# Layer norm's scale through memory: a fused graph network kernel that drops the transposes of h

## The chip, the cores and the metric

One core of one Trainium2 chip. The metric is the device time of one execution in microseconds. All tensors are fp32; matmuls take fp32r operands, and each product is built of three of them (high times high, high times low, low times high).

## The reference, cut to what matters

64 graphs of 128 nodes with 128 channels. `x` is (64, 128, 128), `adj` a mask.

```python
def _layernorm(x, axis=-1, eps=1e-05):
    m = jnp.mean(x, axis=axis, keepdims=True)
    v = jnp.var(x, axis=axis, keepdims=True)
    return (x - m) / jnp.sqrt(v + eps)

h = jnp.maximum(_layernorm(x, axis=-1), 0.0)
return x + gnn(h, adj, ...)

# gnn(x, mask): d = 128
xc = transpose(x, (0, 2, 1))
h = relu(bn1(conv1d(xc, conv1_w, 0)))               # kernel width 1
h = bn2(conv1d(h, conv2_w, 8))                      # 17 taps along the nodes
x_conv = transpose(relu(h + xc), (0, 2, 1))
s = x @ w_se.T + b_se                               # 3 columns
sq = sum(s * s, axis=-1)
A = exp(-(sq[:, :, None] + sq[:, None, :] - 2 s s^T)) * mask
msg = relu(x @ w_msg.T + b_msg)
x_nmp = einsum('bnm,bmd->bnd', A, msg)
gi = concat([x_conv, x_nmp]) @ w_ih.T + b_ih
gh = x @ w_hh.T + b_hh
r = sigmoid(gi_r + gh_r); z = sigmoid(gi_z + gh_z)
n = tanh(gi_n + r * gh_n)
return (1 - z) * n + z * x
```

## The kernel before

The 64 graphs go through in 8 groups of 8 (`NG`, `GB`). Within a group everything is kept turned: channels on the partitions, and 1024 columns (`GW`), node by node with the 8 graphs inside. A group is cut into two halves of 512 columns, the index `c`. Each engine's program is written out by hand, in order, with waits on semaphores; nothing is planned by a compiler. The tail of group g overlaps the head of group g + 1.

Layer norm starts from `xin` (nodes on partitions, 8 tiles of 128x128). VectorE forms `stats` (L715) and `mv` (L722), GpSimd the inverse deviation as a power and its product with the negative mean (`ln_scale`, L348 to L353), ScalarE the normalized rows `hn` in eight passes (`ln_rows`, L449). TensorE turns them (`h_transpose`, L1148, four transposes for each half, into banks 6 and 3 from group 2 on), and ScalarE evicts the banks with a ReLU: once to `h_hi` and once to `hf` (`h_rows`), and by graphs to `hg` (`by_graphs`). VectorE forms `h_lo = hf - h_hi` (`h_low`).

The 17-tap convolution is cut into nine sub-convolutions, `sub_conv(g, 0)` to `sub_conv(g, 8)`, on differences of the input (`level1`, `level2_b`, `level2_u`, in `u`, `vtb`, `vtu`, split to `v_hi` and `v_lo`). ScalarE evicts every third to `mbs` (`m_shared`), VectorE joins the others to it (`join_b`, `add_h`, `add_shared`, `join_y`); their banks are free for the next sub-convolution when that is done. Distances: the three columns of s are split and arranged in `slots` (`distances`, on GpSimd from group 1 on), TensorE turns these (`factor_transposes`, L1189) and multiplies them (`distance`), ScalarE takes the exponential, VectorE applies the mask (`masked`, L888), TensorE gathers (`gather`, L1212). Gates follow, and `update` on VectorE: four passes that also add `x_t`, held in `xt`.

TensorE's order in a group g of the loop:

```python
sub_conv(g, 0); factor_transposes(g); sub_conv(g, 1); distance(g)
sub_conv(g, 2) ... sub_conv(g, 5)
gather(g, 0, 5); h_transpose(g + 1, 0, 6); sub_conv(g, 6)
gather(g, 1, 7); h_transpose(g + 1, 1, 3)
sub_conv(g, 7); sub_conv(g, 8); gates_h(g, 0, ahead)
conv1(g + 1, 0, 0); conv1(g + 1, 1, 7); gates_n(g, 0); gates_xc(g, 0)
gates_h(g, 1, ahead); messages(g + 1); gates_n(g, 1); gates_xc(g, 1)
```

(In group 1 `factor_transposes` and `distance` stand two sub-convolutions later.) The first group also splits the weights into `wt_hi` on ScalarE and `wt_lo` on VectorE, lot by lot, with sums of taps in between, and TensorE runs 25 matmuls on zeros before its first work. All transfers but one are issued by SP in the order of its program.

Of the kernel before, what the change touches and what calls it, by code (L numbers as in the profile page):

```python
# [60 lines left out]
def gnn_kernel(nc, x_nm, x_t, adj_t, w_in, w_conv, w_gate, par_in, row_in, bias_in, out):  # L61
    ctx = ExitStack()
    with ctx:
# [3 lines left out]
        def sem(name):  # L67
# [14 lines left out]
        msg_raw = sb("msg_raw", [P, 9, P])  # L82
# [5 lines left out]
        hn = sb("hn", [P, GB, P])  # L88
# [4 lines left out]
        nmean = sb("nmean", [P, GB])  # L93
        nmr = sb("nmr", [P, GB])
        hf = [sb(f"hf{i}", [P, GW]) for i in range(2)]
# [28 lines left out]
        xt = sb("xt", [P, GW])  # L124
# [6 lines left out]
        w2 = sb("w2", [P, TAPS, P])  # L131
        wg = early[:, 0:9 * P].rearrange("p (k c) -> p k c", c=P)
# [7 lines left out]
        x_landed, xh_landed, wa_landed, w2a_landed, w2b_landed, wg_landed, par_landed, row_landed, bias_landed, xt_landed, mask_landed = (  # L140
            sem("x_landed"), sem("xh_landed"), sem("wa_landed"), sem("w2a_landed"), sem("w2b_landed"),
            sem("wg_landed"), sem("par_landed"), sem("row_landed"), sem("bias_landed"), sem("xt_landed"), sem("mask_landed"))
# [9 lines left out]
        stats_ready, mv_ready, pool_ln, rstd_ready, hn_ready = (  # L152
            sem("stats_ready"), sem("mv_ready"), sem("pool_ln"), sem("rstd_ready"), sem("hn_ready"))
# [124 lines left out]
        def _(sp):  # L278
            sp.dma_start(xin[:, 0:4, :], x_nm[0, :, 0:4, :]).then_inc(xh_landed, 16)
            sp.dma_start(xin[:, 4:8, :], x_nm[0, :, 4:8, :]).then_inc(x_landed, 16)  # L280
# [4 lines left out]
            sp.dma_start(row_raw[0:1, :], row_in).then_inc(row_landed, 16)  # L285
            sp.dma_start(row_raw[32:33, :], row_in).then_inc(row_landed, 16)
            sp.dma_start(bias[:], bias_in).then_inc(bias_landed, 16)
            sp.dma_start(mask[:], adj_t[0]).then_inc(mask_landed, 16)
            for g in range(NG):
                if g + 1 < NG:  # L290

                    sp.wait_ge(hn_ready, NCH * (g + 1))
                    if g < 2:
                        sp.wait_ge(hn_first, g + 2)
                    sp.dma_start(xin[:], x_nm[g + 1]).then_inc(x_landed, 16)

                upto(sp, sum_ready, NCH * g)
                sp.dma_start(xt[:], x_t[g]).then_inc(xt_landed, 16)
                if g > 0:
                    for c in range(NCH):  # L300
# [13 lines left out]
        def _(pool):  # L314
# [27 lines left out]
            def ln_scale(g):  # L342
# [3 lines left out]
                if g == 2:  # L346
                    pool.wait_ge(hn_first, 3)
# [48 lines left out]
        def _(act):  # L396
# [47 lines left out]
            def ln_rows(g):  # L444
# [3 lines left out]
                for j in range(GB):  # L448
                    last = act.activation(hn[:, j, :], xin[:, j, :], ACT.Identity, bias=nmr[:, j:j + 1],  # L449
                                          scale=rstd[:, j:j + 1])  # L450
                    if j % 4 == 3:
                        last.then_inc(hn_ready, 1)
# [1003 lines left out]
```

## Time and profile before

| | us |
|---|---|
| median of 3 runs | 294.5 (294.43 to 295.43) |
| the profiled execution, its time | 294.47 |
| the profiled execution, its span | 292.7 |
| TensorE matmul busy | 281.6 (96%) |
| VectorE busy | 234.9 (80%) |
| ScalarE busy | 181.4 (62%) |
| GpSimd busy | 62.7 (21%) |
| mean granted TensorE clock | 0.996 |

The span is what the profile covers, from the first to the last instruction; the time of an execution has some 1.8 us around it. Busy time of matmuls is latency in a pipeline: the distance between their starts tells what they cost. Group g = 4 starts at 157.02 us with its first sub-convolution.

### The profile page before, as it was taken

How to read it: one execution, taken by the hardware profiler on the slowest of the kernel's cores; microseconds unless marked ns; L12 is line 12 of the kernel's file. 1: busy time of each engine (PE TensorE's matmuls, PEld its weight loads, DVE VectorE, ACT ScalarE, POOL GpSimd, SP SyncE). 2: the span in 40 equal slices, each digit the busy share in tenths (PEclk: the TensorE clock that was granted, in tenths of full speed). 3: DMA queues.
4: the chain of work that ended last, by engine and by line, in shares of the span. 5: the costliest groups of instructions: out<-in, count | busy, mean ns of one | idle time of the engine just before them, and what ended most of it. 6: DMA issues, size and time to landing. Idle time of an engine off the chain costs nothing.

```text
span 292.7 us, 5392 instructions
## 1 busy us (share of the span) xinstructions
PE 281.6 (96%) x1914; PEld 254.6 (87%) x1914; DVE 234.9 (80%) x529; ACT 181.4 (62%) x331; POOL 62.7 (21%) x128
## 2 busy tenths in 40 slices
PE   8779899999999999999999999999999999999993
PEld 6579886999889998899889998899988998899993
DVE  6898988987699668996599776996689966986565
ACT  2776368858656677538765576557674486561362
POOL 7210020540016300460005500361005500140000
PEclk9999999999999999999999999999999999999998
DMA  7700022017000610035000630017000420013001
GB/s 246 301 4 1 0 75 72 0 18 273 2 0 2 223 63 4 0 89 200 0 2 0 168 122 0 2 29 256 5 1 2 143 74 0 0 30 118 2 0 72
DMA packets 6942, 19.03 MB, mean 65 GB/s; under 512 B 898, under 2 KB 1412, under 8 KB 6916
## 3 DMA queue, kind: packets, MB, share of 16 engines
q1 hardware_dynamic: 6772, 18.69, 19.4%
q8 instruction: 15, 0.25, 0.3%
q14 instruction: 11, 0.09, 0.1%
q10 hardware_dynamic: 144, 0.01, 0.0%
HBM read 14.50 MB, written 4.19 MB: 64 GB/s over the span
## 4 chain that ended last, share of the span: by engine, by line
PE 84%; DVE 9%; ACT 3%; issue 1%; POOL 1%; DVEq 0%; POOLq 0%; ACTq 0%
PE ps L1125 23%; PE ps L1127 23%; PE ps L1126 23%; PE ps L1178 4%; PE ps L1212 4%; PE ps L1326 3%; PE ps L1148 2%; DVE wt_lo L735 1%; ACT wt_hi L415 1%; PE ps L1189 1%; PE ps L1202 1%; ACT cp L468 1%; POOL rstd L340 1%; DVE stats L715 1%; DVE vtb L785 1%
## 5 line engine op out<-in xcount | busy, mean ns | idle before, releaser
L1125 PE MATMUL ps<-v_hi,wt_hi 128*128 128x256 f32 x320 | 92.8, 290 | 4.4 <-DVE v_lo L801 3.0
L1127 PE MATMUL ps<-v_hi,wt_lo 128*128 128x256 f32 x320 | 90.0, 281 | 0.0
L1126 PE MATMUL ps<-v_lo,wt_hi 128*128 128x256 f32 x320 | 89.7, 280 | 0.0
L1125 PEld LDWEIGHTS ps<-v_hi,wt_hi 128*128 128x128 f32 x320 | 60.2, 188 | 6.0 <-issue 5.2
L1126 PEld LDWEIGHTS ps<-v_lo,wt_hi 128*128 128x128 f32 x320 | 60.4, 189 | 0.3
L1127 PEld LDWEIGHTS ps<-v_hi,wt_lo 128*128 128x128 f32 x320 | 60.1, 188 | 0.0
L254 POOL CAST slots<-s_sb 128x48 fp32r<-128x48 f32 x7 | 1.6, 228 | 147.3 <-DVE s_sb L873 135.9
L449 ACT ACTIVATE hn<-xin,nmr,rstd 128x128 f32<-128x128 f32 x48 | 19.2, 482 | 13.4 <-POOL nmr L353 13.4
L1125 PE MATMUL ps<-h_hi,wt_hi 128*128 128x512 f32 (+1 forms) x67 | 26.3, 392 | 0.3 <-DVE h_lo L742 0.2
L1127 PE MATMUL ps<-h_hi,wt_lo 128*128 128x512 f32 (+1 forms) x67 | 25.8, 386 | 0.0
L1126 PE MATMUL ps<-h_lo,wt_hi 128*128 128x512 f32 (+1 forms) x67 | 25.8, 385 | 0.0
L566 ACT ACTIVATE gate<-ps,par 128x512 f32<-128x512 f32 x14 | 9.7, 690 | 23.2 <-PE ps L1127 23.2
L844 DVE TENSOR_TENSOR y<-y,mbs 128x512 f32<-128x512 f32 x16 | 11.0, 687 | 14.4 <-ACT mbs L505 14.2
L852 DVE SCALAR_TENSOR_TENSOR y<-ps,par,y 128x256 f32<-128x256 f32 x32 | 14.9, 481 | 7.9 <-PE ps L1127 7.0
L1125 PE MATMUL ps<-n_hi,wt_hi 128*128 128x512 f32 (+1 forms) x51 | 20.0, 392 | 0.0
L1127 PE MATMUL ps<-n_hi,wt_lo 128*128 128x512 f32 (+1 forms) x51 | 19.6, 385 | 0.0
L1127 PE MATMUL ps<-xc_hi,wt_lo 128*128 128x512 f32 (+1 forms) x51 | 19.6, 385 | 0.0
L1126 PE MATMUL ps<-n_lo,wt_hi 128*128 128x512 f32 (+1 forms) x51 | 19.4, 381 | 0.0
L1126 PE MATMUL ps<-xc_lo,wt_hi 128*128 128x512 f32 (+1 forms) x51 | 19.4, 381 | 0.0
L1125 PE MATMUL ps<-xc_hi,wt_hi 128*128 128x512 f32 (+1 forms) x51 | 19.4, 381 | 0.0
L859 DVE SCALAR_TENSOR_TENSOR xc_lo<-y,xc_hi 128x512 fp32r<-128x512 f32 x16 | 10.4, 689 | 10.2 <-ACT xc_hi L554 10.2
L560 ACT ACTIVATE gn<-ps,par 128x512 f32<-128x512 f32 x15 | 10.3, 689 | 11.8 <-PE ps L1127 11.7
(158 smaller groups left out, 644.8 us busy)
## 6 DMA issues: line engine op xcount, KB each, us to landing
mask<-adj_t SPq DMA_DIRECT2D x8, 512.0 KB, 3.3
xt<-x_t SPq DMA_DIRECT2D x8, 512.0 KB, 4.0
out<-gate SPq DMA_DIRECT2D x15, 256.0 KB, 4.1
xin<-x_nm SPq DMA_DIRECT2D x7, 512.0 KB, 3.7
w<-w_conv SPq DMA_DIRECT2D x1, 576.0 KB, 6.7
gate<-w_gate SPq DMA_DIRECT2D x1, 576.0 KB, 7.7
xin<-x_nm SPq DMA_DIRECT2D x2, 256.0 KB, 2.9
w<-w_conv SPq DMA_DIRECT2D x1, 512.0 KB, 5.7
```

The source lines that it names most:

```text
L449: last = act.activation(hn[:, j, :], xin[:, j, :], ACT.Identity, bias=nmr[:, j:j + 1], scale=rstd[:, j:j + 1])
L560: act.activation(gn[c][:], bank(3), ACT.Identity, bias=par[:, HN:HN + 1], scale=0.5).then_inc(ghn_ready, 1)
L566: act.activation(gr[c], bank(4), ACT.Tanh, bias=par[:, HR:HR + 1], scale=0.5).then_inc(r_ready, 1)
L844: dve.tensor_tensor(y_at(s), y_at(s), mbs[1 + s][:].rearrange("p (l b) -> p l b", b=GB).unsqueeze(2).broadcast_to([P, QUART, 2, GB]), ALU. ...
L852: dve.scalar_tensor_tensor(out=at, in0=quarter(1 + t), scalar=par[:, SC2:SC2 + 1], in1=at, op0=ALU.mult, op1=ALU.add).then_inc(y_ready, 1)
L859: dve.scalar_tensor_tensor(out=xc_lo[:, cols(c)], in0=y[:, cols(c)], scalar=0.0, in1=xc_hi[:, cols(c)], op0=ALU.max, op1=ALU.subtract).the ...
L1125: pe.matmul(dst, wt_hi[:, blk, :], hi, start=start, stop=False)
L1126: pe.matmul(dst, wt_hi[:, blk, :], lo, start=False, stop=False)
L1127: return pe.matmul(dst, wt_lo[:, blk, :], hi, start=False, stop=stop)
L1178: last = pe.matmul(ps[:, first + k, i * MW:(i + 1) * MW], hg[:, 3 * k + i, :], w_a[:, P:P + MW], start=not biased, stop=not biased or i == ...
L1212: last = pe.matmul(ps[:, dst, i * P:(i + 1) * P], msg[:, b, :], aff[:, b, :], start=True, stop=True)
L1326: pe.matmul(bank(4), idle[:, 0:P], idle[:], start=True, stop=True)
```

## The change

From group 2 on, h is not turned by TensorE. `x_t` is already turned in memory, so layer norm is applied there: mean and inverse deviation, one value per column, are stored to memory (8 KB, `ln_rows`) by SP and loaded back with the same two rows on all 128 partitions (`col_ln`, 1 MB, in the place of the raw weights). VectorE applies them in four passes for a group (`ln_apply`), behind `masked` and ahead of `add_shared`. ScalarE derives `h_hi` and `hg` from `hf` in place of the eviction of banks. `xt` becomes three buffers, loaded two groups ahead; `xin` too is loaded a group earlier and in another node order, and the statistics of group g + 2 are formed late in group g, around `xc_low`. Groups 0 and 1 keep the old way; `hn` shares the third buffer of `xt`. The raw messages go to `msg` directly.

In the set-up the row of biases is loaded by ScalarE's queue and split first instead of late, one sum of four taps is moved behind two lots, and `v_low_b(0, 0)` goes ahead of `level2_b(0, 0)`. In the last group the second part's output is added and stored ahead of the third's.

```diff
@@ sync
+            def column_rows(g):
+                sp.wait_ge(scale_ready, g - 1)
+                upto(sp, col_landed, 16 * (g - 2))
+                sp.dma_start(ln_rows.rearrange("k (p b) -> p k b", b=GB), scale[:]).then_inc(rows_stored, 16)
+                sp.wait_ge(rows_stored, 16 * (g - 1))
+                sp.wait_ge(wt_lo_ready, LOT_OF_GATES)
+                if g > 2:
+                    sp.wait_ge(hf_ready, NCH * g)
+                sp.dma_start(col_ln, ln_rows.unsqueeze(0).broadcast_to([P, 2, GW])).then_inc(col_landed, 16)
...
+            for g in range(1, NG):
+                sp.wait_ge(out_ready, NCH * (g - 1) + 1)
+                sp.dma_start(out[g - 1, :, cols(0)], ob[0]).then_inc(out_stored[0], 16)
+                if g + 2 < NG:
+                    sp.wait_ge(sum_ready, NCH * g)
+                    sp.dma_start(xts[(g + 2) % 3][:], x_t[g + 2]).then_inc(xt_landed[(g + 2) % 3], 16)
+                sp.wait_ge(out_ready, NCH * (g - 1) + 2)
+                sp.dma_start(out[g - 1, :, cols(1)], ob[1]).then_inc(out_stored[1], 16)
                 if g + 1 < NG:
                     sp.wait_ge(a_ready, NCH * (g + 1))
                     sp.dma_start(mask[:], adj_t[g + 1]).then_inc(mask_landed, 16)
+                if g + 3 < NG:
+                    sp.wait_ge(stats_ready, g + 3)
+                    sp.dma_start(xin[:], x_nm[g + 1]).then_inc(x_landed, 16)
+                if g + 2 < NG:
+                    column_rows(g + 2)
@@ gpsimd
             def ln_scale(g):
-                pool.wait_ge(mv_ready, g - 1)
-                pool.tensor_scalar(vpe[:], mv[:, :, 1], EPS, None, ALU.add).then_inc(pool_ln, 1)
-                pool.tensor_scalar(nmean[:], mv[:, :, 0], -1.0, None, ALU.mult).then_inc(pool_ln, 1)
-                pool.tensor_tensor(rstd[:], vpe[:], neg_half[:], ALU.pow).then_inc(pool_ln, 1)
-                pool.tensor_tensor(nmr[:], nmean[:], rstd[:], ALU.mult).then_inc(rstd_ready, 1)
+                pool.wait_ge(vpe_ready, 2 * (g - 1))
+                upto(pool, rows_stored, 16 * (g - 2))
+                pool.tensor_tensor(scale[:, 1, :], vpe[:], neg_half[:], ALU.pow).then_inc(scale_ready, 1)
...
-            distances(pool, 1)
-            for g in range(2, NG):
-                ln_scale(g)
+            for g in range(1, NG):
+                if g + 1 < NG:
+                    ln_scale(g + 1)
+                    pool.wait_ge(scale_ready, g)
                 distances(pool, g)
@@ scalar
+            def h_high(g, c):
+                act.wait_ge(hf_ready, NCH * g + c + 1)
+                upto(act, z_ps, NCH * (g - 2) + c + 1)
+                act.activation(h_hi[g % 2][:, cols(c)], hf[g % 2][:, cols(c)], ACT.Copy).then_inc(h_hi_ready, 1)
...
                 exponent(g)
+                m_shared(g, 1)
                 if ahead:
-                    ln_rows(g + 1)
-                m_shared(g, 1)
+                    h_high(g + 1, 0)
+                    h_high(g + 1, 1)
+                    graphs_of(g + 1, 0)
                 n_high(g, 0, 5)
                 if ahead:
-                    h_rows(g + 1, 0, 6)
+                    graphs_of(g + 1, 1)
                 m_shared(g, 2)
                 n_high(g, 1, 7)
-                if ahead:
-                    h_rows(g + 1, 1, 3)
-                    by_graphs(g + 1, 0, 6)
-                    by_graphs(g + 1, 1, 3)
@@ vector
             def moments(g):
...
+                dve.tensor_scalar(vpe[:], mv[:, :, 1], EPS, None, ALU.add).then_inc(vpe_ready, 1)
+                upto(dve, rows_stored, 16 * (g - 2))
+                dve.tensor_copy(scale[:, 0, :], mv[:, :, 0]).then_inc(vpe_ready, 1)
+
+            def ln_apply(g, c):
+                dve.wait_ge(col_landed, 16 * (g - 1))
+                dve.wait_ge(xt_landed[g % 3], 16 * (g // 3 + 1))
+                dve.wait_ge(diff_ready, NCH * (g - 2) + c + 1)
+                dst = hf[g % 2][:, cols(c)]
+                dve.tensor_tensor(dst, xts[g % 3][:, cols(c)], col_ln[:, 0, cols(c)],
+                                  ALU.subtract).then_inc(centred, 1)
+                dve.wait_ge(centred, NCH * (g - 2) + c + 1)
+                dve.scalar_tensor_tensor(out=dst, in0=dst, scalar=0.0, in1=col_ln[:, 1, cols(c)], op0=ALU.max,
+                                         op1=ALU.mult).then_inc(hf_ready, 1)
...
-                    if ahead:
-                        ln_stats(g + 1)
-                        moments(g + 1)
                     update(g - 1, 1)
                     join_b(g, 0)
                     join_b(g, 1)
                     add_h(g)
                 masked(g, 0)
                 masked(g, 1)
+                if ahead:
+                    ln_apply(g + 1, 0)
+                    ln_apply(g + 1, 1)
                 add_shared(g, 0)
...
                 join_y(g, 1, 1)
+                if g + 2 < NG:
+                    ln_stats(g + 2)
                 xc_low(g, 0)
                 xc_low(g, 1)
+                if g + 2 < NG:
+                    moments(g + 2)
                 if ahead:
                     level2_b(g + 1, 0)
@@ vector, set-up and group 0 to 1
+            sums_of_four(0)
             lot_low(2)
-            for r in range(2):
-                dve.tensor_tensor(fabk[:, r], raw[:, r], raw[:, r + 2], ALU.add).then_inc(sums_ready, 1)
             dve.wait_ge(pads_set, 6)
+            v_low_b(0, 0)
             level2_b(0, 0)
-            v_low_b(0, 0)
             level2_b(0, 1)
             lot_low(3)
             v_low_b(0, 1)
             lot_low(4)
+            sums_of_four(1)
             level1(0)
...
             ln_stats(2)
+            moments(2)
             level2_b(1, 0)
@@ tensor
                 gather(g, 0, 5)
-                if ahead:
-                    h_transpose(g + 1, 0, 6)
                 sub_conv(g, 6)
                 gather(g, 1, 7)
-                if ahead:
-                    h_transpose(g + 1, 1, 3)
                 sub_conv(g, 7)
```

## Rows read from the trace of the kernel before

**Rows 1.** The page's costliest groups: busy us, mean ns of one, idle before, releaser.
```profile
L449 ACT ACTIVATE hn<-xin,nmr,rstd 128x128 f32<-128x128 f32 x48 | 19.2, 482 | 13.4 <-POOL nmr L353 13.4
```

**Rows 2.** Window of one group: length, then busy us of each engine, clock.
```profile
135.33:169.01 33.68, 33.68 (x234) 30.73 (x233) 27.38 (x61) 21.75 (x39) 8.13 (x15) 1.00 0.20 63
```

**Rows 3.** Timeline of TensorE around a gather: start us, us, engine, line.
```profile
134.27 1.05 PE L1212 MATMUL ps<-aff,msg 128*128 128x128 f32 x8
135.16 0.60 PE L1148 MATMUL ps<-ident,hn 128*128 128x128 f32 x4
135.52 0.36 PE L1125 MATMUL ps<-v_hi,wt_hi 128*128 128x256 f32 x1
```

**Rows 4.** Timeline of TensorE around a gather of the last group.
```profile
269.01 1.05 PE L1212 MATMUL ps<-aff,msg 128*128 128x128 f32 x8
269.81 0.37 PE L1125 MATMUL ps<-v_hi,wt_hi 128*128 128x256 f32 x1
```

**Rows 5.** Timeline of VectorE, end of group 3, group 4; in brackets idle before.
```profile
143.34 1.29 DVE L859 SCALAR_TENSOR_TENSOR xc_lo<-y,xc_hi 128x512 fp32r<-128x512 f32 x2 [1.45 <-ACT xc_hi L554]
145.72 0.78 DVE L785 TENSOR_TENSOR vtb<-cp 128x264 f32<-128x264 f32 x2 [1.09 <-ACT cp L468]
...
152.40 0.68 DVE L914 SCALAR_TENSOR_TENSOR gate<-gate 128x512 f32<-128x512 f32 x1
153.12 0.69 DVE L919 SCALAR_TENSOR_TENSOR gate<-gate,gn 128x512 f32<-128x512 f32 x1
...
158.33 1.64 DVE L715 BATCH_NORM_STATS2 stats<-xin 128x6 f32<-128x128 f32 x8
160.00 0.64 DVE L722 BATCH_NORM_AGGREGATE mv<-stats 128x2 f32<-128x6 f32 x8
...
165.11 1.29 DVE L888 TENSOR_TENSOR aff<-aff,mask 128x512 f32<-128x512 f32 x2
168.87 0.69 DVE L844 TENSOR_TENSOR y<-y,mbs 128x512 f32<-128x512 f32 x1 [2.48 <-ACT mbs L505]
```

**Rows 6.** Timeline of GpSimd in group 4.
```profile
158.15 0.20 POOL L273 CAST slots<-slots 128x16 fp32r<-128x16 f32 x1
...
162.00 1.95 POOL L351 TENSOR_TENSOR rstd<-vpe,neg_half 128x8 f32<-128x8 f32 x1
```

**Rows 7.** Timeline of TensorE in group 4.
```profile
158.78 0.60 PE L1189 MATMUL ps<-ident,slots 128*128 128x128 f32 x4
...
171.96 0.37 PE L1125 MATMUL ps<-v_hi,wt_hi 128*128 128x256 f32 x1
```

**Rows 8.** Timeline of VectorE in the set-up.
```profile
13.09 0.69 DVE L735 TENSOR_TENSOR wt_lo<-gate,wt_hi 128x512 fp32r<-128x512 f32 x1 [0.92 <-ACT wt_hi L415]
13.70 1.28 DVE L995 TENSOR_TENSOR gate<-w 128x512 f32<-128x512 f32 x2
...
15.25 0.42 DVE L801 TENSOR_TENSOR v_lo<-cp,v_hi 128x264 fp32r<-128x264 f32 x1
15.59 1.26 DVE L785 TENSOR_TENSOR vtb<-cp 128x264 f32<-128x264 f32 x1
```

**Rows 9.** Timeline of GpSimd in the set-up.
```profile
15.37 1.19 POOL L387 TENSOR_TENSOR row<-row_raw,row_hi 1x396 fp32r<-1x396 f32 x1 [5.72 <-ACT row_hi L619]
```

**Rows 10.** Timeline of VectorE ahead of and in group 1.
```profile
51.97 0.78 DVE L785 TENSOR_TENSOR vtb<-cp 128x264 f32<-128x264 f32 x2 [0.40 <-ACT cp L468]
...
65.49 1.28 DVE L888 TENSOR_TENSOR aff<-aff,mask 128x512 f32<-128x512 f32 x2
```

**Rows 11.** Timeline of VectorE at the end.
```profile
289.57 0.76 DVE L955 TENSOR_TENSOR gate<-gate,gn 128x256 f32<-128x256 f32 x2
```

**Rows 12.** DMA issues by line: count, KB each, median us to landing.
```profile
xin<-x_nm SPq DMA_DIRECT2D x7, 512.0 KB, 3.7
...
gate<-w_gate SPq DMA_DIRECT2D x1, 576.0 KB, 7.7
...
par<-par_in ACTq DMA_DIRECT2D x1, 7.0 KB, 2.8
```

More of the change, by code:

```diff
@@ L87, in gnn_kernel @@
         xin = sb("xin", [P, GB, P])
-        hn = sb("hn", [P, GB, P])
         stats = sb("stats", [P, GB, 6])
@@ L122, in gnn_kernel @@
         n_lo = sb("n_lo", [P, P, GB], F32R)
-        xt = sb("xt", [P, GW])
+        xts = [sb(f"xt{i}", [P, GW]) for i in range(3)]
+        hn = xts[2][:].rearrange("p (j c) -> p j c", c=P)
         gn = [sb(f"gn{c}", [P, CW]) for c in range(NCH)]
@@ new lines, in _ @@
+            sp.wait_ge(hn_ready, NCH)
+            sp.wait_ge(hn_first, 2)
+            sp.dma_start(xin[:], x_first[1]).then_inc(x_landed, 16)
+            for g in range(2):
+                sp.dma_start(xts[g][:], x_t[g]).then_inc(xt_landed[g], 16)
+            sp.wait_ge(a_ready, NCH)
+            sp.dma_start(mask[:], adj_t[1]).then_inc(mask_landed, 16)
+            sp.wait_ge(hn_ready, 2 * NCH)
+            sp.wait_ge(hn_first, 3)
+            sp.dma_start(xin[:], x_nm[0]).then_inc(x_landed, 16)
@@ L306, in _ @@
                     sp.dma_start(mask[:], adj_t[g + 1]).then_inc(mask_landed, 16)
-            for count, p in enumerate((0, 2, 1)):
-                sp.wait_ge(out_ready, LAST + count)
+                if g + 3 < NG:
[3 more added lines that the diff above has]
+                    column_rows(g + 2)
+            for p in range(3):
+                sp.wait_ge(out_ready, LAST + p)
                 sp.dma_start(out[NG - 1, :, PART_COLS[p]], part_of(ob, p)).then_inc(out_stored[min(p, 1)], 16)
@@ L738, in h_low @@
             def h_low(g, c):
-                dve.wait_ge(hf_ready, NCH * g + c + 1)
+                if g == 1:
+                    dve.wait_ge(hf_ready, NCH * g + c + 1)
+                else:
+                    dve.wait_ge(h_hi_ready, NCH * (g - 2) + c + 1)
                 upto(dve, z_ps, NCH * (g - 2) + c + 1)
@@ L1248, in gates_h @@
                 if c == 0:
-                    if ahead and g > 0:
-                        pe.wait_ge(hg_ready, NCH * (g + 1) + NCH)
-                    else:
-                        pe.wait_ge(e_ready, g + 1)
+                    pe.wait_ge(e_ready, g + 1)
                     if g == 0:
@@ L1452 @@
     out = nc.dram_tensor("out", (NG, P, GW), F32, kind="ExternalOutput").ap()
-    gnn_kernel(nc, *args, out)
+    ln_rows = nc.dram_tensor("ln_rows", (2, GW), F32, kind="Internal").ap()
+    gnn_kernel(nc, *args, ln_rows, out)
     got = run_bass_kernel_spmd(nc, [arrays], core_ids=[0]).results[0]["out"]
```

105 lines of the change are left out of this document (49 added, 56 removed).

## The prediction, made before the result

> **What bounds the kernel now.** I read the windows by group first. In a full group TensorE is busy for all 33.68 us of 33.68, and five windows in a row say so, the first being 33.88 us long [rows 2]. VectorE has 27.38 us of work in it and ScalarE 21.75. From about 54 us to 288 us nothing but matmuls sets the time, so in that stretch only matmuls taken away are a gain, and work given to another engine costs nothing until it makes TensorE wait. Then the TensorE timeline, for what a transpose really costs: the busy time of a matmul is its pipelined latency (273 ns for a transpose), so I take differences of start times. Then the timelines of VectorE, GpSimd and ScalarE over one group, for how early each result lies before the matmul that needs it. At last the first 54 us and the last 5, where TensorE does wait.
>
> **Transposes removed.** Between the start of a gather and the start of the sub-convolution behind it lie 1.25 us (134.27 to 135.52) where four transposes stand between them [rows 3], and 0.80 us (269.01 to 269.81) in the last group, which has none [rows 4]. So four transposes cost 0.45 us, two such sets a group 0.90 us, and groups 2 to 7 are the ones that lose them: 12 x 0.45 = 5.4 us. This is the term that I trust most.
>
> **VectorE's new work.** `ln_apply` is four passes over 128x512. A pass follows an independent one after 0.61 us and a dependent one after 0.72 us (152.40 to 153.12) [rows 5]; two pairs make 4 x 0.61 + 2 x 0.11 = 2.7 us. The two small operations behind the aggregates are some 0.3 us. VectorE goes to about 27.4 + 3.0 = 30.4 us of 32.8: 93%, not yet the bound, so it is a question of places.
>
> - *Before `add_shared`.* VectorE sat idle there for 2.48 us, because ScalarE was at the eight normalizing passes (482 ns each) when it should have evicted `mbs` [rows 1, 5]. Those passes are gone, so `mbs` is there early. The statistics and aggregates (1.64 + 0.64 us) leave the stretch ahead of it, but the joins wait for the third sub-convolution, so `masked` ends only 0.4 us earlier, at 166.0 in the time of rows 5. With `ln_apply` it is 168.7, `add_shared` and the first join follow by about 169.9. The sub-convolution that waits for this join started at 171.96 [rows 7] and will want to start 0.90 us earlier, at 171.1. That leaves 1.2 us: no stall.
> - *Statistics at the end of the group.* They go into the idle 1.45 us ahead of `xc_low`, and the aggregates with the two small operations (0.95 us) into the 1.09 us ahead of `level2_b` [rows 5]. The first overflows by 0.2 us. Both gaps are waits for TensorE's results passed on by ScalarE, which come 0.9 us earlier with everything else, so they stay as long. So `level2_b` is within 0.1 us of where it would be.
> - *What that would cost if it were late.* From `level2_b` to the raw messages VectorE never waits, and GpSimd's factors come behind them: the last of these ended at 158.35, and the transposes of the factors start at 158.78 [rows 6, 7]. The margin is 0.43 us. It is the narrowest in the group; every tenth beyond it is paid in each of 5 groups.
>
> **GpSimd.** The power (the inverse root) now stands before `distances(g)`, where GpSimd had been idle; it needs 1.95 us. The row at 162.00 shows such a power beside VectorE's passes of two inputs, of which the one at 153.12 and its neighbours just before, in every group, take 0.68 to 0.69 us with or without a power beside them [rows 5, 6]. Yet the start of the kernel has the other case: VectorE's 264-element subtraction took 1.26 us at 15.59, where two of its kind at 145.72 took 0.78 us together, until GpSimd's operation begun at 15.37 was over [rows 5, 8, 9]. The Trainium skill (SBUF — State Buffer, "SBUF: two separate sides") has it that a GpSimd operation and a VectorE one with two SBUF inputs lock each other out for a whole instruction; the second pair of rows agrees with that, the first doesn't. By the rule the sum would be worse by the last rival below.
>
> **The way through memory.** Store of 8 KB, wait, load of 1 MB (two rows of 4 KB on 128 partitions). No row shows either. The store: 2.8 us, by the load of the parameters, the nearest in size. The load: 512 KB land in 3.7 us, so at least 3.7 and, if all of that scaled, 7.4; the weights' 576 KB needed 7.7 us in the crowded start, so at most 15.4 [rows 12]. I take 7.4. By the formula in the Trainium skill (DMA: Bandwidth & Descriptors, "Anatomy of one DMA") the load would be an estimated 4.4 us, which would change nothing here. From the aggregates (178.4 in the time of rows 5) the chain is 1.95 + 2.8 + 7.4 = 12.2 us, and the columns are needed one group later at 166.0 + 32.8 = 198.8: 20.4 us. It is hidden by 8 us, and even with the upper end (20.2) just so. SP's queue stands behind the store's wait, but next in it is the output of the first half, which is ready only some 8 us after the aggregates and has a group's time to go out. Cost 0.
>
> **ScalarE.** It loses 8 x 482 ns and one of two evictions per half, and so has some 5 us less per group. Its new place in the order puts `n_high` behind both `h_high` and one `graphs_of`, so behind the end of `ln_apply` at 168.7 by about 1.7 us (three passes at the pace of VectorE's, two of them once the last half is there): 170.4, when VectorE has just done the joins that stand ahead of `n_low`. Cost 0; were it late, `n_low` and the second `add_shared` would follow, with 1.2 us of room.
>
> **The first 54 us.** Ahead of the first sub-convolution TensorE waits 3 us for `v_low_b(0, 0)`, ended at 15.67 [rows 8]. One sum of four (0.64 us) moves into the idle 0.92 us ahead of 13.09, the other behind, and `v_low_b` ahead of a level: it can end at 14.1, so 1.5 us earlier. What follows is VectorE's chain, which at the factors of group 0 (about 29 us) gains what VectorE itself gains: 0.64 us from the idle gap and 0.84 us from the blocked subtraction, since GpSimd's row operation goes earlier. There it may hit one of the splits of h, up to the same 0.84 us. Between 0.6 and 1.5 I take 1.0 us; the idle 0.92 us would absorb a part of such a hit.
>
> **Group 1 is different.** The aggregates of group 2 come before `level2_b(1)`, which waited only 0.40 us for its input: 1.0 - 0.4 = 0.6 us later [rows 10]. In this group the update stands behind the joins, and `masked` ended at 66.8; now at 67.4, with `ln_apply` 70.1, with `add_shared` and the join 71.2. The sub-convolution that needs it stood at 171.96 - 101.24 = 70.72 (three windows, 33.88 + 2 x 33.68) and wants to start at 69.9. So TensorE waits about 1.3 us, once. It leaves VectorE 0.5 us late at the next `level2_b`, over the margin of 0.43: another 0.1 to 0.3. Its columns would land near 54.6 + 2.8 + 7.4 = 64.8, before 67.4; at the upper end they'd be 5 us late, once.
>
> **The end.** The last two additions ran together (0.76 us from 289.57) after the last product [rows 11]. Now one runs while ScalarE still forms the last tanh: 0.35 us less, and its store is issued earlier.
>
> **Sum.** - 5.4 (transposes) - 1.0 (start) + 1.3 + 0.2 (group 1 and behind) - 0.35 (end) = - 5.25 us. The profiled execution has a span of 292.7 and a time of 294.47, 1.8 us around it, and the median is 294.5: so 294.5 - 5.25, rounded 289.2 us.
>
> **Rivals.**
> - *Only the stall of group 1 and the start come out otherwise* (that is the forecast's own spread): without the stall and with 1.5 us at the start 287.2; with the start at 0, 290.3. Forecast with this spread: chance 0.62.
> - *VectorE too full.* At 93% the margin of 0.43 us is used up in each group, say because `xc_low` and the aggregates come 0.7 us late rather than 0.1. For it: no idle time between 145.72 and 158.3. Against it: the two gaps just hold the moved work. Price 0.3 to 0.6 us in 5 groups: 290.7 to 292.2. Chance 0.20.
> - *The whole gain is given back*: VectorE sets the pace at about 33.6 us. It would need 3 us more of work per group than I count. 293.5 to 295: chance 0.05.
> - *The columns come late* (slower than before). The 1 MB load reads the same 8 KB 128 times; should that be slow, `ln_apply` waits with `add_shared`, the joins and the sub-convolution behind it. It begins to cost at 20.4 + 1.2 us of chain, so a load of 16.8 us, and decides for slower at 1.1 us more, at 18 us. At 20 us: 6 x 3.2 - 5.25 gives 308. Against it: 3.7 us for 512 KB. Chance 0.06.
> - *The power holds VectorE* (slower too). 1.95 us more ahead of `level2_b`, less 0.43 of margin, is 1.5 us in each of 6 groups: 289.2 + 9 = 298. This is what the rule of the Trainium skill (SBUF — State Buffer, "SBUF: two separate sides") would make of it. Against it speaks the row at 162.00, under whose 1.95 us the update ran at its usual pace and `masked` came no later than the joins allowed. Chance 0.04.
> - *Transposes don't pay* (their 0.45 us is a switch between weights that stays): 294. Rows 3 and 4 compare the same neighbours, so 0.03.
>
> A measurement of this kernel can tell about 0.5% (1.5 us) from no change. Faster by more: the first two cases and a part of the others, 0.85. Within: 0.06. Slower: 0.09. The range reaches to the ends of the first two: 287.0 to 292.2.
>
> **What would show it.** Period 32.8 us a group with TensorE without a gap; no wait of the transposes of the factors on `slots`; a wait of about 1.3 us on `y` near 69 us; first sub-convolution near 14.3; four `ln_apply` passes of 0.68 us with no idle time on `col_ln`, and a load of the columns under 8 us. I would be wrong if the period came out at 33.2 or more, or if the load took over 16 us.

## The result, and the profile after

The changed kernel takes 289.6 us (median of 5 runs, 289.56 to 289.69) against 294.5 us (5 runs, 294.43 to 295.43): the ratio is 0.9825, with a 95% interval of 0.9808 to 0.9841. The profiled execution took 289.65 us with a span of 287.5 us, so 2.15 us lie around the span, where it was 1.77 us before. I had predicted 289.2 us.

The windows by group come first, answering to [rows 2]: length, busy us of PE, PEld, DVE, ACT and POOL, then the granted clock, the DMA share and GB/s. The first starts with the sub-convolution behind the first gather of group 1 and runs into group 2; the other two start some 0.2 us after a first gather starts, and each spans one full group.

```profile
66.50:100.56 34.06, 32.60 (x221) 29.32 (x220) 31.24 (x69) 19.59 (x30) 5.68 (x12) 1.00 0.31 106
100.56:133.34 32.78, 32.78 (x226) 29.87 (x226) 29.95 (x67) 18.90 (x30) 5.68 (x12) 1.00 0.29 95
133.34:166.13 32.79, 32.79 (x226) 29.87 (x226) 29.95 (x67) 18.91 (x30) 5.68 (x12) 1.00 0.28 98
```

TensorE has no gap in a full group, and the group is 32.78 us long instead of 33.68: 0.90 us less, eight matmuls fewer. VectorE went from 27.38 to 29.95 us of work and ScalarE from 21.75 to 18.90. The first window is 1.28 us longer than the others, and that isn't yet all that was lost in it, for it also begins 0.64 us later in its group than it ends in the next: from the sub-convolution behind the first gather of group 1 (66.50) to that of group 2 (101.20) it is 34.70 us, 1.92 more than in a full group. The timeline of TensorE shows where its waits are; in brackets the idle time before a matmul and what ended it.

```profile
14.28 0.36 PE L1190 MATMUL ps<-v_hi,wt_hi 128*128 128x256 f32 x1 [1.41 <-DVE v_lo L858]
...
67.99 1.06 PE L1274 MATMUL ps<-aff,msg 128*128 128x128 f32 x8
69.73 0.39 PE L1190 MATMUL ps<-v_hi,wt_hi 128*128 128x256 f32 x1 [0.69 <-DVE y L909]
...
90.11 0.28 PE L1192 MATMUL ps<-v_hi,wt_lo 128*128 128x256 f32 x1
91.16 0.66 PE L1251 MATMUL ps<-ident,slots 128*128 128x128 f32 x4 [0.77 <-POOL slots L279]
...
156.74 0.65 PE L1251 MATMUL ps<-ident,slots 128*128 128x128 f32 x4
...
165.96 1.06 PE L1274 MATMUL ps<-aff,msg 128*128 128x128 f32 x8
166.78 0.36 PE L1190 MATMUL ps<-v_hi,wt_hi 128*128 128x256 f32 x1
```

The last pair answers to [rows 3]: a gather and the sub-convolution behind it start 0.82 us apart, where it was 1.25. The wait at 69.73 is the stall foreseen for group 1. By differences of starts it is 69.73 - 67.99 - 0.81 = 0.93 us (the printed 0.69 counts from the modelled end of the gather). The wait at 91.16, in group 2, comes on top; by starts it too is 91.16 - 90.11 - 0.12 = 0.93 us, and the printed 0.77 counts from a modelled end. (0.12 us is the usual distance between two such starts.) At 156.74 the profile shows no wait of the transposes of the factors.

VectorE in group 4, answering to [rows 5]:

```profile
140.37 1.64 DVE L747 BATCH_NORM_STATS2 stats<-xin 128x6 f32<-128x128 f32 x8
141.92 1.28 DVE L916 SCALAR_TENSOR_TENSOR xc_lo<-y,xc_hi 128x512 fp32r<-128x512 f32 x2
143.11 0.64 DVE L756 BATCH_NORM_AGGREGATE mv<-stats 128x2 f32<-128x6 f32 x8
...
143.94 0.77 DVE L842 TENSOR_TENSOR vtb<-cp 128x264 f32<-128x264 f32 x2
144.64 0.70 DVE L834 TENSOR_TENSOR u<-cp 128x536 f32<-128x536 f32 x1
...
153.92 1.33 DVE L870 TENSOR_TENSOR v_lo<-vtu,v_hi 128x528 fp32r<-128x528 f32 x2
...
155.91 0.69 DVE L961 TENSOR_TENSOR gn<-ps,gn 128x512 f32<-128x512 f32 x1
...
164.05 0.68 DVE L773 TENSOR_TENSOR hf<-xt,w 128x512 f32<-128x512 f32 x1
164.77 0.69 DVE L776 SCALAR_TENSOR_TENSOR hf<-hf,w 128x512 f32<-128x512 f32 x1
...
167.51 0.88 DVE L909 SCALAR_TENSOR_TENSOR y<-ps,par,y 128x256 f32<-128x256 f32 x2
169.09 0.69 DVE L951 TENSOR_TENSOR n_lo<-ps,n_hi 128x512 fp32r<-128x512 f32 x1 [0.70 <-ACT n_hi L582]
...
170.56 0.70 DVE L901 TENSOR_TENSOR y<-y,mbs 128x512 f32<-128x512 f32 x1 [0.18 <-ACT mbs L541]
```

The idle times of 1.45 and 1.09 us are filled by the statistics and the aggregates. `ln_apply` (L773 and L776; the columns stand in `w`) doesn't wait for them. The 0.70 us at 169.09 are new, and ScalarE's timeline has their cause:

```profile
166.83 0.63 ACT L481 ACTIVATE h_hi<-hf 128x512 fp32r<-128x512 f32 x1 [0.70 <-DVE hf L776]
167.37 1.21 ACT L486 ACTIVATE hg<-hf 128x512 f32<-128x512 f32 x1
168.49 0.57 ACT L582 ACTIVATE n_hi<-ps 128x512 fp32r<-128x512 f32 x1
168.96 1.20 ACT L486 ACTIVATE hg<-hf 128x512 f32<-128x512 f32 x1
170.06 0.46 ACT L541 ACTIVATE mbs<-ps,par 128x256 f32<-128x256 f32 x1
```

`graphs_of` (L486) takes 1.2 us, and one stands ahead of `n_high(g, 0)`, the other ahead of `m_shared(g, 2)`.

GpSimd in group 4: its power, and four of its last six operations on the factors.

```profile
144.11 1.78 POOL L382 TENSOR_TENSOR scale<-vpe,neg_half 128x8 f32<-128x8 f32 x1 [20.22 <-DVE scale L764]
...
154.69 0.65 POOL L272 CAST slots<-slots 128x48 fp32r<-128x48 f32 x1
155.41 0.53 POOL L274 CAST slots<-sq 128x8 fp32r<-128x8 f32 x1
155.87 0.23 POOL L275 CAST slots<-slots 128x48 fp32r<-128x48 f32 x1
...
156.47 0.20 POOL L279 CAST slots<-slots 128x16 fp32r<-128x16 f32 x1
```

The DMA issues: count, KB each, median us to landing.

```profile
w<-ln_rows SPq DMA_DIRECT2D x6, 1024.0 KB, 4.7
```

The end on VectorE, where one output addition now runs ahead of the last tanh's product [rows 11]:

```profile
284.07 0.42 DVE L1012 TENSOR_TENSOR gate<-gate,gn 128x256 f32<-128x256 f32 x1
284.42 0.42 DVE L1005 TENSOR_TENSOR gn<-gn,hf 128x256 f32<-128x256 f32 x1
284.87 0.42 DVE L1012 TENSOR_TENSOR gate<-gate,gn 128x256 f32<-128x256 f32 x1
```

### The profile page after: what moved, and what is told of

Read it like the earlier page. It is cut to its first block, busy times and chain, and to the rows that moved or that the text cites. A ratio compares the mean times of both kernels' runs of the same rounds, so it can differ in the third digit from the quotient of the medians.

```text
span 287.5 us, 5282 instructions
## 1 busy us (share of the span) xinstructions
PE 276.3 (96%) x1866; PEld 248.8 (87%) x1866; DVE 249.8 (87%) x565; ACT 164.5 (57%) x271; POOL 49.7 (17%) x110
## 4 chain that ended last, share of the span: by engine, by line
PE 67%; DVE 17%; issue 7%; ACT 5%; POOL 2%; DMA 1%; DVEq 0%; ACTq 0%; POOLq 0%
PE ps L1190 20%; PE ps L1192 19%; PE ps L1191 19%; PE ps L1274 4%; PE ps L1240 3%; DVE stats L747 2%; DVE wt_lo L789 2%; ACT wt_hi L448 1%; POOL rstd L376 1%; PE ps L1251 1%; DMA xin<-x_first 1%; DVE aff L945 1%; DVE v_lo L870 1%; DVE y L890 1%; PE ps L1264 1%
## 5 line engine op out<-in xcount | busy, mean ns | idle before, releaser
L382 POOL TENSOR_TENSOR scale<-vpe,neg_half 128x8 f32<-128x8 f32 x6 | 10.6, 1767 | 110.5 <-DVE scale L764 110.5
L541 ACT ACTIVATE mbs<-ps,par 128x256 f32<-128x256 f32 x24 | 12.0, 501 | 14.9 <-DVE y L890 14.1
L481 ACT ACTIVATE h_hi<-hf 128x512 fp32r<-128x512 f32 x12 | 7.6, 634 | 17.8 <-DVE hf L776 17.8
L1274 PE MATMUL ps<-aff,msg 128*128 128x128 f32 x128 | 16.8, 276 | 0.0
```

The lines of the kernel that those rows point to most:

```text
L382: pool.tensor_tensor(scale[:, 1, :], vpe[:], neg_half[:], ALU.pow).then_inc(scale_ready, 1)
L481: act.activation(h_hi[g % 2][:, cols(c)], hf[g % 2][:, cols(c)], ACT.Copy).then_inc(h_hi_ready, 1)
L541: act.activation(mbs[i][:], ps[:, 0, 0:QW], ACT.Identity, scale=par[:, SC2:SC2 + 1], **bias).then_inc(mbs_ready, 1)
L1274: last = pe.matmul(ps[:, dst, i * P:(i + 1) * P], msg[:, b, :], aff[:, b, :], start=True, stop=True)
```

## The experiments

Theory: TensorE sets the time, the transposes are worth 0.45 us a set, and the small rest of the time is in stalls that VectorE's and ScalarE's order in group 1 make. Rivals: the transposes cost nothing of their own, and the time came from elsewhere; VectorE is already the bound; the way through memory matters.

**1. The transposes put back.** Changed kernel, four transposes of the unit matrix into the bank behind each gather of groups 1 to 6; nobody reads them.

```diff
                 gather(g, 0, 5)
+                if ahead:
+                    turn_nothing(6)
                 sub_conv(g, 6)
                 gather(g, 1, 7)
+                if ahead:
+                    turn_nothing(3)
```

> The changed kernel with four transposes put back behind each of the two gathers of groups 1 to 6, of the identity by itself into the banks that the old ones wrote; nothing reads them, so only TensorE's work returns. Theory (TensorE sets the pace, 0.45 us for four transposes): the period of a full group goes from 32.78 back to 33.68 us and the time rises by close to 5.4 us, less what VectorE's one-off lateness in groups 1 and 2 (0.93 and 0.77 us of waiting on TensorE) gets back because each group gives VectorE 0.9 us more: 294.0 to 295.0 us. Rival (VectorE at 29.95 us of work already sets the period, the transposes would be hidden): under 291 us.

Measured: 293.9 us (293.8 to 294.06), ratio to before 0.998 (0.9972 to 0.9991). The transposes are 4.3 us of the 4.9, and the rival falls. That it isn't 5.4: the stall on `y` in group 1 (0.93 us) vanished, since the transposes give VectorE the time that it lacked; the one on `slots` in group 2 stayed at 0.77 us. A full group took 33.64 us, 0.86 more than in the changed kernel, and five of them make the 4.3 us.

**2. The order alone.** The kernel before with only the reordered set-up and end.

```diff
             lot_low(1)
+            sums_of_four(0)
             lot_low(2)
-            level2_b(0, 0)
             v_low_b(0, 0)
+            level2_b(0, 0)
...
             part_keep(1)
+            part_out(1)
             part_keep(2)
             part_out(2)
-            part_out(1)
```

> The kernel before with nothing but the reordered set-up (row of biases on ScalarE's queue and split first, one sum of taps later, v_low_b ahead of level2_b) and the reordered end; layer norm as before. Theory: the 1.4 us that the changed kernel is ahead at 48 us and the 0.4 us at the end come from these edits alone: 292.5 to 292.9 us, first convolution matmul near 14.3 us. Rival (the head start is given back at the next wait that VectorE's chain causes): 294.0 us or more.

Measured: 292.7 us (292.66 to 292.82), ratio 0.9941 (0.9926 to 0.9956): 1.7 us, close to the 1.9 that the traces of the whole change say (start 1.42, end 0.44).

**3. `n_high` ahead of the first `graphs_of`.** ScalarE's order in the changed kernel, for the wait at 169.09.

```diff
                     h_high(g + 1, 1)
-                    graphs_of(g + 1, 0)
                 n_high(g, 0, 5)
                 if ahead:
+                    graphs_of(g + 1, 0)
                     graphs_of(g + 1, 1)
```

> The changed kernel with one exchange in ScalarE's order in every group: n_high(g, 0) ahead of the first graphs_of instead of behind it (1.2 us earlier). Theory: VectorE's wait of 0.70 us for n_hi is what makes the rest of its group late and has used up the margin of the factors on GpSimd (156.67 against 156.74); with the exchange the wait shrinks below 0.2, the factors end 0.3 to 0.5 us ahead of their transposes, and the wait of 0.77 us for slots in group 2 goes down to 0.2 or so: 289.0 to 289.3 us. Rival (the 0.77 us belong to group 1's late ln_apply alone, whatever n_high does): 289.6 us, no change.

Measured: 289.5 us (289.52 to 289.55), which is no change. The wait for `n_hi` is gone, but both `graphs_of` now stand ahead of `m_shared(g, 2)`, and VectorE waits there instead:

```profile
170.43 0.69 DVE L901 TENSOR_TENSOR y<-y,mbs 128x512 f32<-128x512 f32 x1 [0.92 <-ACT mbs L541]
```

**4. `ln_apply` behind the joins, in group 1 alone,** against the stall on `y`.

```diff
-                if ahead:
+                if ahead and g > 1:
                     ln_apply(g + 1, 0)
                     ln_apply(g + 1, 1)
                 add_shared(g, 0)
                 join_y(g, 0, 0)
                 join_y(g, 0, 1)
+                if g == 1:
+                    ln_apply(g + 1, 0)
+                    ln_apply(g + 1, 1)
                 n_low(g, 0, 5)
```

> The changed kernel with ln_apply of group 2 moved behind add_shared and the first two joins, in group 1 only. Theory A (VectorE is simply full between 50 and 91 us, the wait of 0.93 us on y is only the first place where it shows): the wait on y goes, but h_lo of group 2 or the factors come late by about as much: 289.4 to 289.8 us, with a new wait of TensorE of 0.5 to 1.1 us between 73 and 92 us. Theory B (it is a matter of this one order): the time falls by the 0.93 us, to 288.6 to 288.8 us.

Measured: 291.3 us (291.18 to 291.34), slower than either theory. The stall on `y` is gone as meant, but `n_high(1, 0)` stands behind `h_high` on ScalarE, so VectorE waits for ScalarE, which waited for VectorE. VectorE's timeline:

```profile
72.22 0.69 DVE L951 TENSOR_TENSOR n_lo<-ps,n_hi 128x512 fp32r<-128x512 f32 x1 [2.29 <-ACT n_hi L582]
```

and TensorE's:

```profile
76.06 0.50 PE L1193 MATMUL ps<-h_hi,wt_hi 128*128 128x512 f32 x1 [1.29 <-DVE h_lo L799]
...
92.67 0.66 PE L1254 MATMUL ps<-ident,slots 128*128 128x128 f32 x4 [1.25 <-POOL slots L279]
```

These are two stalls of 1.3 us as printed, where the changed kernel has 0.69 us on `y` and 0.77 us on `slots`: an instruction moved on one engine needs the other engine's order to go with it.

**5. Both `graphs_of` behind everything that VectorE waits for.**

```diff
-                    graphs_of(g + 1, 0)
                 n_high(g, 0, 5)
-                if ahead:
-                    graphs_of(g + 1, 1)
                 m_shared(g, 2)
                 n_high(g, 1, 7)
+                if ahead:
+                    graphs_of(g + 1, 0)
+                    graphs_of(g + 1, 1)
                 ghn_rows(g, 0)
```

> The changed kernel with both graphs_of of ScalarE moved behind n_high(g, 0), m_shared(g, 2) and n_high(g, 1), in every group. The run with n_high alone ahead only moved VectorE's wait from n_hi (0.70 us) to mbs (0.92 us), since the graphs_of passes of 1.2 us each then stood ahead of m_shared. Theory: with both behind, VectorE's two waits (0.70 and 0.20 us) nearly go, level2_b is bound by the eviction of conv1 again, the factors are some 0.3 us earlier in a full group and 0.7 to 0.9 us in group 2, whose wait of 0.77 us on slots goes: 288.8 to 289.1 us. Rival (ScalarE's order is not what makes VectorE late in group 2): 289.5 us or more.

Measured: 288.5 us (288.47 to 288.54), ratio 0.9796 (0.9781 to 0.9811), 1.1 us under the changed kernel and a little better than expected. The stall in group 2 is gone, which is 0.93 us by starts, and a full group takes 32.75 us for 32.78; the stall on `y` stays (0.68 us at 69.69). The factors end at 155.39 and their transposes start at 155.69: the margin in a full group is 0.3 us.

**6. `ln_apply` late and `n_high` early.** Experiment 5, and in group 1 `n_high(1, 0)` ahead of `h_high`, `ln_apply(2)` behind `n_low(1, 0)`.

```diff
                 m_shared(g, 1)
+                if g == 1:
+                    n_high(g, 0, 5)
...
                 n_low(g, 0, 5)
+                if g == 1:
+                    ln_apply(g + 1, 0)
+                    ln_apply(g + 1, 1)
```

> The order of the run before it, and in group 1 alone n_high(1, 0) ahead of h_high, and on VectorE the first shared add, the first two joins and n_low(1, 0) ahead of ln_apply of group 2. Theory: the wait of 0.93 us on y goes, and this time nothing on ScalarE holds n_hi back, so it doesn't come back at h_lo as the 1.3 us did when ln_apply alone was moved: 287.9 to 288.4 us, one wait of at most 0.5 us on slots in group 2 left. Rival (VectorE is full there and any order gives the wait back): within 0.2 us of the run before it.

Measured: 289.1 us (289.02 to 289.13). Missed: the stall on `y` is gone, and a larger one on `slots` is there instead:

```profile
90.61 0.66 PE L1257 MATMUL ps<-ident,slots 128*128 128x128 f32 x4 [1.23 <-POOL slots L279]
```

VectorE waited 0.46 us at 71.67 for `m_shared(1, 2)`, which stood behind the second `h_high`.

**7. The aggregates of group 2 late.** Experiment 6, with `moments(2)` back at the head of group 1 on VectorE, and GpSimd's power behind `distances(1)`.

```diff
             ln_stats(2)
-            moments(2)
             level2_b(1, 0)
...
                 if g == 1:
+                    moments(2)
                     join_b(g, 0)
```

> The kernel before this one, with the aggregates of group 2 moved behind reset(0, 1), into VectorE's idle 1.24 us, and distances(1) ahead of the power on GpSimd. Theory: the sub-convolution behind the factors' transposes of group 1 is no longer 0.37 us late, for its mbs comes 0.9 us earlier; the columns of group 2 land near 67.4 us, when ln_apply wants them at about 67.2: 0 to 0.4 us less than the kernel before this one. Rival (the columns land later than that): equal or slower, with a wait of VectorE on the columns.

Measured: 289.1 us (289.07 to 289.32), as experiment 6. The stall on `slots` is 1.26 us, and `ln_apply` had to wait for its columns, 0.29 us at 68.01. But the sub-convolution behind the factors' transposes of group 1 starts 0.36 us after them, where it is 0.72 us in experiment 6: the theory holds there, and the gain is lost again by group 2.

**8. One pass more on VectorE.** Changed kernel, the first pass of `level1` doubled in groups 2 to 7 (0.72 us each). It measures how full VectorE is.

```diff
+                if g > 1:
+                    dve.tensor_tensor(u[:, 0, 0:n, :], cp[:, every(0, n), :], cp[:, every(1, n), :],
+                                      ALU.subtract).then_inc(twice, 1)
+                    dve.wait_ge(twice, g - 1)
                 dve.tensor_tensor(u[:, 0, 0:n, :], cp[:, every(0, n), :], cp[:, every(1, n), :], ALU.subtract)
```

> The changed kernel with the first pass of level1 done twice in groups 2 to 7 (0.72 us more for VectorE in each, the result the same). Theory from the trace after (the factors end 0.07 us before their transposes start, so VectorE has no room ahead of them although it is busy for only 29.95 of 32.78 us): groups 2 to 6 pay 0.65 us each and group 7 some 0.3: 292.5 to 293.5 us, the period 33.4 us. The prediction's own margin (0.43 us less 0.1) would make it 5 x 0.4 = 2 us: 291.6. Rival (VectorE's 2.8 us of idle time a group absorb a pass): 289.6 to 289.9 us.

Measured: 293.5 us (293.45 to 293.6), 3.9 us more. The waits of TensorE, in us in total, times and longest:

```profile
PE ps L1256 <- POOL slots L280: 3.8, 6, 1.2
```

The printed waits of full groups are 0.57 us (at 125.36 and 158.91), but they count from modelled ends. By starts these transposes are 33.55 us apart, where the changed kernel has 32.78: the whole pass is paid in a full group, a little more than the 0.65 us of the theory. There is no room ahead of the factors, though VectorE is idle for 9% of the group.

**9. Group 1 untangled.** Experiment 6, and in group 1 `m_shared(1, 2)` and `n_high(1, 1)` ahead of the second `h_high`.

```diff
                 if ahead:
                     h_high(g + 1, 0)
+                if ahead and g > 1:
                     h_high(g + 1, 1)
...
                 m_shared(g, 2)
                 n_high(g, 1, 7)
+                if g == 1:
+                    h_high(g + 1, 1)
```

> The kernel with ln_apply of group 2 behind the first joins and n_high ahead (289.1 us), and in group 1 alone m_shared(1, 2) and n_high(1, 1) ahead of the second h_high too. There VectorE waited 0.46 us for mbs behind it; from its first pass to the factors of group 2 it has no other idle time, and TensorE waited 1.23 us for the factors. Theory (VectorE is full from 62 to 90 us, so each idle tenth of it is a tenth for TensorE): the 0.46 us come off that wait: 288.5 to 288.7 us. Rival (the wait on slots is GpSimd's own chain): 289.1 us.

Measured: 288.7 us (288.54 to 288.84), ratio 0.9796 (0.9781 to 0.981), not told apart from experiment 5. It has no stall on `y` but 0.80 us on `slots` at 90.26; experiment 5 has it the other way round, and by starts both are about 0.9 us. I read this as VectorE and GpSimd being some 0.9 us behind in that stretch, where the order only says at which of the two places TensorE meets it.

**10. The kernel before without the transposes.** The two `h_transpose` calls of groups 2 to 7 are taken out, and ScalarE's evictions behind them read what the bank then holds: the h of these groups is left out of the computation. All else, the eight normalizing passes too, stays.

```diff
                 gather(g, 0, 5)
-                if ahead:
-                    h_transpose(g + 1, 0, 6)
                 sub_conv(g, 6)
                 gather(g, 1, 7)
-                if ahead:
-                    h_transpose(g + 1, 1, 3)
```

> The kernel before with the transposes of h for groups 2 to 7 left out and nothing in their place: ScalarE evicts what lies in the banks, after the gather in their stead, so h of these groups is not computed. All else as before, VectorE's work too. Theory (a set of four costs 0.45 us of TensorE, and VectorE has its old room): the period goes to 32.78 us, the time down by 5.4 us: 289.0 to 289.2 us. Rival (a part of the 0.45 us is the switch of weights and comes back at the next matmul): above 290 us.

Measured: 291.2 us (291.04 to 292.1), ratio 0.9879 (0.9863 to 0.9896): 3.4 us less where 5.4 were expected. ScalarE's timeline ahead of group 3's gathers shows what came instead:

```profile
131.69 3.19 ACT L450 ACTIVATE hn<-xin,nmr,rstd 128x128 f32<-128x128 f32 x8 [2.68 <-POOL nmr L353]
134.79 0.45 ACT L508 ACTIVATE mbs<-ps,par 128x256 f32<-128x256 f32 x1
```

And TensorE's:

```profile
134.36 1.05 PE L1215 MATMUL ps<-aff,msg 128*128 128x128 f32 x8
135.38 0.36 PE L1128 MATMUL ps<-v_hi,wt_hi 128*128 128x256 f32 x1
...
136.88 1.05 PE L1215 MATMUL ps<-aff,msg 128*128 128x128 f32 x8
137.69 0.37 PE L1128 MATMUL ps<-v_hi,wt_hi 128*128 128x256 f32 x1
```

The second gather has 0.81 us behind it, as without transposes; the first has 1.02. Its sub-convolution waits for `mbs`, which ScalarE takes out of PSUM only once its eight passes over h are done, at 135.24. In the kernel before, the transposes covered just that. It costs 0.2 us in groups 2 to 6 and 0.62 us in group 1 (67.81 to 69.24), in sum 1.6 of the 2.0 us missing; 0.4 us I can't place. (The profiled execution took 292.1 us: it started group 0's gather 1.1 us later than the kernel before, with a granted clock of 0.51 from 15 to 20 us. Between that gather and the last one of group 7 it took 232.45 us against 235.88 of before, and these 3.4 us are what the median shows too.)

**11. The columns loaded behind the first output,** the changed kernel with the load 5.0 us later in a full group (152.53 for 147.52). In group 1, where that output is ready anyway, it is issued as early as before.

```diff
                 sp.dma_start(out[g - 1, :, cols(0)], ob[0]).then_inc(out_stored[0], 16)
+                if g + 1 < NG:
+                    column_load(g + 1)
```

> The changed kernel with the 1 MB load of the columns issued behind the store of the first half's output instead of ahead of it, some 4.9 us later in a full group. Theory (loaded some 11 us before use in a full group, 6 us in group 1, where the store is ready anyway): no change, 289.5 to 289.7 us. Rival (the load is late already in places): over 290 us.

Measured: 289.7 us (289.65 to 289.87), no change.

**12. The columns loaded behind both outputs.**

```diff
                 sp.dma_start(out[g - 1, :, cols(1)], ob[1]).then_inc(out_stored[1], 16)
                 if g + 1 < NG:
+                    column_load(g + 1)
+                if g + 1 < NG:
                     sp.wait_ge(a_ready, NCH * (g + 1))
```

> As the run before it, but behind the store of the second half's output: 12.9 us later in a full group, 10 in group 1. Landing then near 165.3 where ln_apply started at 164.05, and 4 us late in group 1. Theory (VectorE has no room ahead of the factors, as the run with one more pass showed): VectorE waits 1.2 us on the columns in each of 5 groups and 4 us once, and nearly all of it reaches TensorE: 297 to 300 us. Rival (the room of 1.1 us ahead of the join hides it): about 293 us, the 4 us of group 1 alone.

Measured: 316.6 us (314.36 to 317.15), ratio 1.073 (1.069 to 1.077), much slower than either. VectorE's timeline in group 3:

```profile
148.34 0.69 DVE L777 TENSOR_TENSOR hf<-xt,w 128x512 f32<-128x512 f32 x1 [3.82 <-DMA w<-ln_rows]
```

TensorE's timeline behind that:

```profile
152.35 0.39 PE L1194 MATMUL ps<-v_hi,wt_hi 128*128 128x256 f32 x1 [2.64 <-DVE y L913]
```

The windows around it, columns as above:

```profile
148.00:150.00 2.00, 1.71 (x15) 1.52 (x14) 1.62 (x3) 0.20 (x1) 0.00 (x0) 1.00 0.04 16
150.00:152.00 2.00, 0.00 (x0) 0.00 (x0) 1.85 (x4) 1.30 (x3) 0.00 (x0) 1.00 0.00 0
152.00:156.00 4.00, 3.65 (x22) 3.65 (x23) 3.19 (x7) 3.23 (x5) 0.00 (x0) 0.71 0.00 0
156.00:160.00 4.00, 4.00 (x18) 3.36 (x18) 4.00 (x14) 1.90 (x4) 0.00 (x0) 0.86 0.00 0
```

The DMA issues of this kernel:

```profile
w<-ln_rows SPq DMA_DIRECT2D x6, 1024.0 KB, 7.7
```

Two things were mis-sized. The load takes 7.7 us here and not 4.7: `xt` (512 KB) and an output (256 KB) are issued 1.8 and 0.5 us ahead of it, so three transfers are under way together. VectorE waits 24.1 us for it in six groups (7.3 the longest, in group 1), and TensorE 19 us for `y` behind that, in five of them. And in the stretch behind the wait TensorE's granted clock is 0.71, then 0.86: parts of it at 1.2 GHz instead of 2.4; behind the longest wait, in group 1, it is 0.50 from 77 to 81 us. The span is 27.3 us longer; the 8 us beyond the waits I put down to such stretches (mean clock 0.961 against 0.996), without having tried it apart.

## Why the prediction was right, point by point

- *Transposes, - 5.4 us.* Right: 0.90 us a group in six groups, and a gather followed after 0.82 us. But the step had a condition that I didn't name. Experiment 10 shows that this gain is there in full only if ScalarE's passes go too: without that, 3.4 us. That the rest comes with the passes is read from the period of the changed kernel; no run takes the passes away alone. I had looked at what the transposes cost and not at what they covered.
- *VectorE.* The added work came to 29.95 - 27.38 = 2.6 us a group, predicted 3.0. The places were right: the two gaps took the statistics and the aggregates, and `ln_apply` the wait for `mbs`. The join that the sub-convolution at 169.08 needs, the first of the two begun at 167.51, ended at about 168.0: 1.1 us ahead, predicted 1.2.
- *ScalarE, cost 0.* This step failed. I gave three passes the pace of VectorE's and took `graphs_of` for one of them; it takes 1.2 us. So `n_low` waited 0.70 us and the second `add_shared` 0.18 us in each group. That used up the margin at the factors: 156.67 to 156.74 is 0.07 us, where I had counted about 0.33. A full group paid only some 0.03 us for it (32.78 us against 32.75 in experiment 5), by luck of those 0.07 us; group 2, already late, paid 0.93 us. I had also counted some 5 us less work a group, and it was 2.85 (21.75 to 18.90): the eviction saved for each half went to the slower `graphs_of`.
- *The narrowest place.* I named the factors, with a margin of 0.43 us before. Experiment 8 confirms the place: 0.72 us of work more, and a period longer by all of it. The rival "VectorE too full" was nearer than its chance of 0.20.
- *GpSimd's power.* Right: VectorE's passes of two inputs at 143.94 and 144.64, under the power begun at 144.11, took 0.77 (for two) and 0.70 us, as without it. The lock-out rule of the Trainium skill (SBUF — State Buffer, "SBUF: two separate sides") isn't borne out by these rows; its price, 9 us, didn't come (that is the last rival but one of the list, which the text on GpSimd calls the last). I overlooked the other direction, where the rows do agree with it. GpSimd's short operations on the factors took 0.53 to 0.75 us each from 153.31 to 155.9, while VectorE ran passes with two inputs in SBUF; the cast of 128x48 at 154.69 took 0.65 us, under the two passes begun at 153.92. A cast of the same size took 0.23 us at 155.87, beside the pass begun at 155.91, which reads PSUM (`ps`). It is so in each of groups 2 to 6; in group 7, where another pass with two inputs in SBUF runs beside this second cast, it takes 0.70 us. No run here tries it apart. So how long the factors take depends on which VectorE passes run beside them, at the narrowest place of the group.
- *The way through memory.* Cost 0, right: columns of group 5 are issued at 147.52 and, by the median of 4.7 us, are there at 152.2, 11.8 us ahead of 164.05. I took 7.4 us for the load, and scaling by size was too much; the store took 1.6 us (145.92 to 147.52 between the two issues), where I took 2.8. The estimate of 4.4 us by the Trainium skill (DMA: Bandwidth & Descriptors, "Anatomy of one DMA") was nearer, though that section gives its formula for transfers that GpSimd issues, and this one is issued by SP. Experiments 11 and 12 bound the slack in place of arguing it.
- *The start, - 1.0 us.* Mis-sized: 1.42 us. The first sub-convolution began at 14.28 for 15.82 before, and 1.42 us of that 1.54 were left at the first convolution of group 1 (48.04 for 49.46). I had set aside up to 0.84 us for GpSimd's row operation hitting another pass; the pass under it took 0.83 us, some 0.15 more than its kind.
- *Group 1 and behind, + 1.5 us.* Mis-sized: 0.93 us on `y` (predicted 1.3), 0.93 us on `slots` in group 2 (predicted 0.1 to 0.3), and 0.37 us that I hadn't seen, behind the transposes of the factors of group 1 (59.33 to 60.06 between starts, 0.36 elsewhere). There VectorE too waits for ScalarE, in its row at 59.94. Experiment 7, with the aggregates and the power later, has 0.36 us between those starts: the 0.37 us are the price of their place. In sum 2.23 us, less 0.18 that the kernel before lost in group 1 (its two gathers start 2.93 us apart there and 2.75 in a full group) and this one doesn't: 2.05 us. The stall on `slots` is ScalarE's order again: with `graphs_of` last, it is gone.
- *The end, - 0.35 us.* 0.44 us.

The row of VectorE's timeline of the changed kernel that the last point but one speaks of:

```profile
59.94 0.88 DVE L880 SCALAR_TENSOR_TENSOR mb<-ps,par,mbs 128x256 f32<-128x256 f32 x2 [1.24 <-ACT mbs L541]
```

Sum: - 5.4 - 1.42 + 2.05 - 0.44 = - 5.2 us, which is the difference of the spans (292.7 and 287.5). That this is also the predicted - 5.25 is in part luck: the start and the end gave 0.5 us more than I said, and group 1 and what is behind it cost 0.55 us more. The 0.4 us between 289.2 and 289.6 lie outside the span, in the 2.15 us around it that were 1.77 before; why they grew, no run here shows.

## What to carry to other kernels

Before counting an instruction's removal as a gain, ask which later wait it covers: the transposes were worth their full price only together with the normalizing passes that stood behind them. When passes move to another engine, write down their place in every engine's order, and put those that only a late matmul needs behind those on which the fullest engine waits; that alone gave 1.1 us. The narrowest margin of a steady loop is found by adding one pass and seeing how much of it is paid.

## What the runs showed of the hardware

ScalarE's pass that spreads 128x512 by graphs took 1.20 us when it read `hf` in SBUF with a stride of eight elements, where the same pass from PSUM took 0.62 us before (its line has 16 of them, 620 ns each), and a copy of 128x512 without a stride from SBUF took 0.63 us. A load that gives the same 8 KB to 128 partitions (1 MB written) landed in 4.7 us alone and in 7.7 us beside two others. GpSimd's cast of 128x48 took 0.65 us beside VectorE's passes with two inputs in SBUF and 0.23 us beside one that reads PSUM. A wait of 2.9 us on TensorE (by starts) was in one group of experiment 12 followed by a stretch at a granted clock of 0.71, and the next group's, of 2.5 us (185.83 to 189.15), by one at 1.00.
